# Working out the flags of irregular rows before the slot indices, and leaving their places out of the gather

## The reference

```python
h = jnp.maximum(_layernorm(x, axis=-1), 0.0)
s_i = h @ attn[:d]
s_j = h @ attn[d:]
e = jax.nn.leaky_relu(s_i + s_j.T, negative_slope=0.2)
e = e + jnp.where(adj > 0, jnp.float32(0.0), neg_inf)   # adj: 8192 x 8192 int32
alpha = jax.nn.softmax(e, axis=1)
return x + alpha @ h
```

## Time and profile before

| | |
|---|---|
| median of 3 runs | 822.78 us (821.7 to 823.1) |
| span of the profiled execution | 819.9 us |
| around the span, to the median | 2.9 us |
| DMA engines' share, 60 to 100 us and 600 to 700 us | 1.01 |
| busy: VectorE, ScalarE, GpSimd, TensorE | 615, 534, 505, 380 us |
| bytes moved by DMA | 301.59 MB |

### The profile page before, as it was taken

The page is one execution under the profiler, slowest core; times in us unless marked ns, Lnnn a source line. Parts: engine busy times, 40 slices in busy tenths (PEclk is TensorE's granted clock), DMA queues, the critical chain, the costliest instruction groups (busy, mean ns, idle before and its releaser), DMA issues.

```text
span 819.9 us, 6412 instructions
## 1 busy us (share of the span) xinstructions
PE 379.5 (46%) x1378; PEld 171.4 (21%) x1378; DVE 615.3 (75%) x2028; ACT 534.3 (65%) x410; POOL 505.0 (62%) x526
## 2 busy tenths in 40 slices
PE   1546334444444344344343434444434546653765
PEld 1322011111111011111111101111111215431654
DVE  6898298677768667797778666697689799897831
ACT  4975676676676666766766666676676677764620
POOL 6720777755457767665547677555557667655771
PEclk9776665555555555555555555655555556766768
DMA  8999999999999999999999999999999999981210
GB/s 341 402 411 415 392 404 408 406 414 413 409 407 410 408 405 410 406 410 410 412 406 407 408 406 407 411 410 413 412 413 409 408 411 407 409 348 43 53 37 4
DMA packets 39719, 301.59 MB, mean 368 GB/s; under 512 B 10682, under 2 KB 17149, under 8 KB 22272
## 3 DMA queue, kind: packets, MB, share of 16 engines
q1 hardware_dynamic: 24032, 277.04, 83.1%
q0 software_dynamic: 15360, 23.88, 8.5%
q10 hardware_dynamic: 288, 0.26, 0.1%
HBM read 303.76 MB, written 8.98 MB: 381 GB/s over the span
## 4 chain that ended last, share of the span: by engine, by line
DMA 76%; issue 11%; DVE 5%; ACT 4%; PE 3%; POOL 0%; DVEq 0%; ACTq 0%
DMA adj_ring<-in_adj_dram 75%; ACT sign_ring L613 3%; PE words L1442 2%; DVE one_hot L724 1%; ACT h_all L625 1%; PE words L1406 1%; DMA x_all<-in_x_dram 1%; PE words L1366 0%; DVE cand L769 0%; DVE adj_ring L1142 0%; DVE adj_ring L1138 0%; DVE adj_ring L1146 0%; PE words L1516 0%; POOL out_dram L562 0%; ACT terms L620 0%
## 5 line engine op out<-in xcount | busy, mean ns | idle before, releaser
L613 ACT ACTIVATE sign_ring<-adj_ring,half_neg 128x4096 fp8e3<-128x4096 int32 x128 | 474.9, 3710 | 217.1 <-DMA adj_ring<-in_adj_dram 215.4
L521 POOL DMA_INDIRECT near<-h_table,near_id x384 | 391.8, 1020 | 235.4 <-issue 122.8
L1366 PE MATMUL words<-sign_ring,pack_w 128*128 128x512 bf16 x512 | 225.2, 592 | 354.8 <-ACT sign_ring L613 354.8
L769 DVE MAX8 cand<-words 128x8 f32<-128x256 f32 x256 | 90.9, 417 | 115.4 <-PE words L1366 115.4
L1366 PEld LDWEIGHTS words<-sign_ring,pack_w 128*128 128x128 bf16 x512 | 55.0, 127 | 521.9 <-ACT sign_ring L613 451.6
L954 DVE TENSOR_REDUCE sums<-terms 128x128 f32<-128x1024 f32 x58 | 112.2, 1934 | 2.0
L532 POOL DMA_INDIRECT near_m<-h_table,id_m x64 | 64.5, 1008 | 19.5 <-issue 19.2
L949 DVE TENSOR_TENSOR terms<-near,weight 128x512 f32<-128x512 f32 (+1 forms) x87 | 73.4, 871 | 0.0
L1357 PE MATMUL words<-place,place_w 128*128 128x512 bf16 x128 | 62.1, 586 | 3.6 <-DVE key L861 3.6
L1392 PEld LDWEIGHTS listing<-cand,one_hot 128*128 128x128 f32 x128 | 33.6, 321 | 10.9 <-issue 7.7
L1347 PE MATMUL listing<-h_all 128*1 128x128 f32 x128 | 19.1, 322 | 22.8 <-ACT h_all L625 22.8
(11 more groups left out here) (271 smaller groups left out, 524.3 us busy)
## 6 DMA issues: line engine op xcount, KB each, us to landing
adj_ring<-in_adj_dram SPq DMA_DIRECT2D x128, 2048.0 KB, 24.6
near<-h_table,near_id POOLq DMA_INDIRECT x384, 6.4
h_table<-h_all POOLq DMA_DIRECT2D x4, 1056.0 KB, 14.7
x_all<-in_x_dram SPq DMA_DIRECT2D x4, 1024.0 KB, 9.4
out_dram<-x_all SPq DMA_DIRECT2D x30, 128.0 KB, 23.9
near_m<-h_table,id_m POOLq DMA_INDIRECT x64, 6.4
out_dram<-x_all ACTq DMA_DIRECT2D x2, 128.0 KB, 2.5
adj_ring<-h_table SPq DMA_DIRECT2D x1, 132.0 KB, 2.6
```

What stands on the lines that cost most here:

```text
L521: pool.indirect_dma_start(out=near[:, p % RING, k, :], out_offset=None, in_=table, in_offset=bass.IndirectOffsetOnAxis(ap=near_id[:, p % I ...
L613: nc.scalar.activation(bytes_of, adj_ring[:, n % HALVES, :].rearrange("p (d r i) -> p d r i", r=2, i=WORDS), ACT.Sign, bias=half_neg[:, :] ...
L769: last = nc.vector.max(out=cand[:, p % 2, t % 2, 8 * q:8 * q + 8], in_=words[t % 3][:, q * PART:(q + 1) * PART])
L1366: last = nc.tensor.matmul(at[:, k * BANK:(k + 1) * BANK], pack_w[:, d, :], twins[:, o + k * BANK:o + (k + 1) * BANK], start=False, stop=(d ...
```

## The change

`find_pair` now ends with `missing`. The flag part comes right behind it, then `drop_listed`, which multiplies both rows' codes by `keep` (0 for a flagged row, 1 for any other), and then `place_pair`, which is the rest of the old `find_pair`: merge and indices. The counting of flags is a function of its own, `count_pair`, and stays where `flag_pair` stood, behind the first half of the sums. In pair 0 the three new calls stand in front of the bounds of the lone rows.

```diff
-        FIND = 16
-        FLAG = 6
+        FIND = 17
+        FIND_CODES = 10
+        FLAG = 7
+        FLAG_KEEP = 5
...
                 dve.wait_ge(find, f + 9)
+                nc.vector.tensor_reduce(missing[:, :], invalid[:, p % IDS, :].rearrange("p (a k) -> p a k", a=2),
+                                        AX.X, ALU.add).then_inc(find, 1)
+
+            def drop_listed(p):
+                dve.wait_ge(flagging, FLAG * p + FLAG_KEEP)
+                nc.vector.tensor_tensor(
+                    best_f[:, :].rearrange("p (a k) -> p a k", a=2), best_f[:, :].rearrange("p (a k) -> p a k", a=2),
+                    keep[:, :].unsqueeze(2).broadcast_to([P, 2, 2 * OWN]), ALU.mult).then_inc(find, 1)
+
+            def place_pair(p):
+                f = FIND * p + FIND_CODES
+                dve.wait_ge(find, f + 1)
                 nc.vector.tensor_tensor(best[:, 1, :], best[:, 1, :], best[:, 3, ::-1], ALU.max).then_inc(find, 1)
...
                 nc.vector.tensor_tensor(near_id[:, p % IDS, :], offset[:, :], unused[:, :], ALU.add) \
                     .then_inc(near_id_ready, 1)
-                nc.vector.tensor_reduce(missing[:, :], invalid[:, p % IDS, :].rearrange("p (a k) -> p a k", a=2),
-                                        AX.X, ALU.add).then_inc(find, 1)
...
             def flag_pair(p):
                 f = FLAG * p
                 ts = slice(2 * p, 2 * p + 2)
-                dve.wait_ge(find, FIND * p + FIND)
-                if p > 0:
-                    dve.wait_ge(flags_ready, p)
+                dve.wait_ge(find, FIND * p + FIND_CODES)
                 dve.wait_ge(signed, 4 * p + 4)
...
                 dve.wait_ge(flagging, f + 4)
+                nc.vector.tensor_scalar(keep[:, :], listable[:, ts], 0.0, None, ALU.is_ge).then_inc(flagging, 1)
                 if p >= 2:
                     dve.wait_ge(ranked, p - 1)
...
+            def count_pair(p):
+                f = FLAG * p
+                if p > 0:
+                    dve.wait_ge(flags_ready, p)
...
                 find_pair(p)
+                flag_pair(p)
+                drop_listed(p)
+                place_pair(p)
                 if p < PAIRS - 1:
                     for g in mixes:
                         weigh_mix(g)
                         add_row(g, 0)
-                flag_pair(p)
+                count_pair(p)
```

More of the change, by code:

```diff
@@ L161, in graph_attention_kernel @@
         lacking = sb("lacking", [P, 2], fp32)
+        keep = sb("keep", [P, 2], fp32)
         curve = sb("curve", [P, 2], fp32)
@@ L804, in find_pair @@
                 dve.wait_ge(find, f + 9)
+                nc.vector.tensor_reduce(missing[:, :], invalid[:, p % IDS, :].rearrange("p (a k) -> p a k", a=2),
[8 more added lines that the diff above has]
+                dve.wait_ge(find, f + 1)
                 nc.vector.tensor_tensor(best[:, 1, :], best[:, 1, :], best[:, 3, ::-1], ALU.max).then_inc(find, 1)
-                dve.wait_ge(find, f + 10)
+                dve.wait_ge(find, f + 2)
                 nc.vector.tensor_scalar(power[:, :], best_f[:, 0:SLOTS].bitcast(i32), EXPONENT, None,
@@ L810, in find_pair @@
                                                ALU.is_lt, ALU.mult).then_inc(find, 1)
-                dve.wait_ge(find, f + 11)
+                dve.wait_ge(find, f + 3)
                 nc.vector.tensor_scalar(chunk[:, :], power[:, :], 2.0 / 3 / 2 ** MANTISSA, -2.0 / 3 * FIRST,
                                         ALU.mult, ALU.add).then_inc(find, 1)
-                dve.wait_ge(find, f + 12)
+                dve.wait_ge(find, f + 4)
                 nc.vector.scalar_tensor_tensor(unused[:, :], unused[:, :], 1.0, best_f[:, 0:SLOTS],
                                                ALU.add, ALU.add).then_inc(find, 1)
-                dve.wait_ge(find, f + 13)
+                dve.wait_ge(find, f + 5)
                 nc.vector.scalar_tensor_tensor(offset[:, :], chunk[:, :], float(WORDS), power[:, :].bitcast(fp32),
                                                ALU.mult, ALU.subtract).then_inc(find, 1)
-                dve.wait_ge(find, f + 15)
+                dve.wait_ge(find, f + 7)
                 nc.vector.tensor_tensor(near_id[:, p % IDS, :], offset[:, :], unused[:, :], ALU.add) \
                     .then_inc(near_id_ready, 1)
-                nc.vector.tensor_reduce(missing[:, :], invalid[:, p % IDS, :].rearrange("p (a k) -> p a k", a=2),
-                                        AX.X, ALU.add).then_inc(find, 1)
             def flag_pair(p):
@@ L853, in flag_pair @@
                                             ALU.add).then_inc(flagging, 1)
-                dve.wait_ge(flagging, f + 6)
+                dve.wait_ge(flagging, f + FLAG)
                 nc.vector.tensor_tensor(prior[:, p % 2, 1:2], prior[:, p % 2, 0:1], flag[:, p % 2, 0:1], ALU.add) \
@@ L1215, in _ @@
             find_pair(0)
+            flag_pair(0)
+            drop_listed(0)
+            place_pair(0)
             dve.wait_ge(extreme_spread, 1)
@@ L1227, in _ @@
                                            ALU.is_lt, ALU.max).then_inc(bounds_ready, 1)
-            flag_pair(0)
+            count_pair(0)
             for p in range(1, PAIRS):
```

## The result

The changed kernel takes 823.62 us (median of 20 runs, 821.20 to 825.08), the kernel before 822.22 (20 runs, 819.68 to 824.23). The ratio is 1.0018 with an interval of 1.001 to 1.0026: slower by 0.18%, 1.4 us. 820.9 was forecast, in a range of 819.2 to 823.9. So the time is within the range, but a gain of 1.9 us was forecast and a small loss came. The profiled execution of the changed kernel took 822.9 us with a span of 821.1, where that of before has a span of 819.9: 1.2 us more.

A forecast was written before the change was run, and what follows sets the result against it. The prediction took full DMA engines to bound the stream, followed by a tail of some 70 us. Stream -3.3 and tail +1.4 made -1.9 us: 820.9 against the median of 822.8, range 819.2 to 823.9.

The forecast's parts named there:

- What bounds the stream, and which bytes leave it: Stream up to about 747 us: DMA engines are full; 2610 flagged rows' records, 1.38 MB, leave before it ends.
- The rival in which a flagged row's own first slot is still gathered: Stream: 405 of 2610 records stay, gain 2.8 us, total 821.4; within the 0.22 for less gain or VectorE late.
- The slower rival: Stream: gathers' bytes do not pace it, so only the tail's 1.4 to 2.2 us remain; 824.2 to 825.0, chance 0.14.
- The size of the stream's gain: Stream: leaving out 2610 records brings its end 3.3 us earlier, with 2.2 and 4.0 as bounds.
- The move: Pair's index chain: flags ahead of the merge delay near_id by 1.4 us, hidden in pairs 0 to 30, uncovered in 31.
- VectorE's cover: End of the stream: VectorE's idle time covers two added operations, 0.3 to 0.4 us a pair; about 2.4 us left.
- They are level at 775.58 now, so the tail grows by 1.4: Pair 31: gather chain 1.4 us later, VectorE chain 0.3, so the tail grows by 1.4; bounds 0.3 and 2.2.
- The stall of one gather: Pair 31's last gather took 1.81 us, the first 0.99; without that stall 0.8 us comes back.
- Theory A: From the experiments, tail: pair 31's twelfth gather meets the lone rows' loop's three loads, so the tail grows beyond the move.
- rival B: From the experiments, tail: the last gather lands late by itself, through left-out indices or chance; order costs its plain shift.
- the case in which the stream gains little or nothing: Stream: removed gather bytes do not bring loads forward; the lower edge of this slower case set the range's end, 823.9.

The follow-up runs named there:

- e2_pair31_old: The change in pairs 0 to 30 only, pair 31 in the old order with all places gathered; 819.40 us, ratio 0.9965 to the kernel before.
- e9_drop_more: e2_pair31_old with all rows' places also left out in seven pairs, 6463 records more; 812.80 us, ratio 0.9895 to the kernel before.
- e7_old31_gate: e2_pair31_old with SyncE's wait for pair 31's gathers directly ahead of the lone rows' loop; 818.15 us, ratio 0.9955 to the kernel before.
- e3_order31: The kernel before with the flags ahead of the places in pair 31 alone, nothing left out; 826.19 us, ratio 1.0045.
- e5_order_all: The kernel before with the new order in all pairs, nothing left out of the gathers; 824.69 us, ratio 1.0035.
- e10_before_gate: Control: the kernel before with SyncE's wait for pair 31's gathers ahead of the loop's loads; 821.49 us, ratio 0.9997.
- e6_gate_late: The changed kernel with SyncE's wait for pair 31's gathers behind the reading of the loop's bounds; 820.27 us, ratio 0.9979 to the kernel before.
- e1_gate: The changed kernel with SyncE held until pair 31's last gather lands, before reading the loop's bounds; 821.03 us, ratio 0.9975 to the kernel before.
- e8_gate_mid: The changed kernel with only the loop's adjacency and x tile loads waiting for pair 31's gathers; 821.26 us, ratio 0.9992 to the kernel before.
- e11_gate_x: The changed kernel with only the loop's x tile load waiting for pair 31's gathers; 823.29 us, ratio 1.0018 to the kernel before.

## Why the prediction was wrong, step by step

- **What bounds the stream, and which bytes leave it: right.** q0 22.42 MB and the whole 300.13 were forecast as 22.4 and 300.1. The rival in which a flagged row's own first slot is still gathered falls by the same row: an index below zero moves no record either. The slower rival, in which the gathers' bytes do not pace the stream, falls by e2_pair31_old and e9_drop_more.
- **The size of the stream's gain: perhaps too large, and not settled.** 3.3 us were forecast, 1.3 ns a record, with bounds of 2.2 and 4.0. e2_pair31_old and e7_old31_gate, which change little but the stream, gain 2.9 and 3.7 by their ratios. The other readings are lower. The seven kernels that leave out these records and no others (the changed one among them) have their last sign between 743.75 and 745.15, 744.62 on average; the four that leave out none (before, e3_order31, e5_order_all, e10_before_gate) have it between 746.16 and 747.39, 746.83 on average: 2.2 us. At e9_drop_more's 0.95 ns it would be 2.5. The ratios of e3_order31 and e5_order_all to the changed kernel, which share its meeting, make it 2.2 and 1.4, or 2.5 and 1.7 with the 0.3 us of the two added operations. The 3.06 us at the last maxima of the changed kernel's own profile come near the 3.3 only because 0.85 of them are the clock. Why the loads take longer when the records are gone stays open.
- **The move: right to the hundredth.** 1.4 us forecast, 1.40 in the rows. The sum by the rule of the Trainium skill (VectorE: DVE Perf Modes, The TRN2 errata) had been about 0.6; the trace of the changed kernel does not agree either, each of the small operations takes 0.16 to 0.18 us. The same section of the Trainium skill says that the row with the 58 cycles falls short for a single operation and that its measured fixed term is about 150 cycles, an estimate of 0.16 us at the 0.96 GHz that it gives, and with that the trace agrees; the prediction left it out. That the move is hidden in pairs 0 to 30 is shown by e5_order_all against e3_order31.
- **VectorE's cover: right in that VectorE did not become the bound; its size by luck.** About 2.4 us were worked out to be left ahead of the last tile, and the row has 2.48. But 0.85 of the difference to the 3.72 before is the clock: where the packing ran at the 1.2 GHz level and the order is the same, 3.41 to 3.71 are left (e6_gate_late, e1_gate, e8_gate_mid). The prediction also saw no idle time between 640.03 and 707.64, where the kernel before has 0.55 us at 685.57, and expected none to be left at the release of 707.64, where the changed kernel still has 0.85:

```profile
685.57 1.43 DVE L769 MAX8 cand<-words 128x8 f32<-128x256 f32 x4 [0.55 <-PE words L1366]
```
```profile
705.43 1.43 DVE L772 MAX8 cand<-words 128x8 f32<-128x256 f32 x4 [0.85 <-PE words L1389]
```
- **"They are level at 775.58 now, so the tail grows by 1.4", with bounds of 0.3 and 2.2: this step failed.** From the last maxima to the scores it grew by 4.9 us: 1.4 for the move and 3.5 for the landing. From the last sign to the end of the span it is 76.4 us instead of 72.9, 3.4 more where 1.4 was forecast. The stall of one gather that the prediction reckoned with came back, in the eleventh instead of the twelfth, and pushed the twelfth, so it is the same in both. e1_gate and e6_gate_late bring the landing back to 1.60 and 1.74, and they are 3.5 and 3.2 us faster than the changed kernel by their ratios. With the loads out of the way the tail grows by 1.40 and 1.53, as forecast. Theory A is shown; rival B falls with them, since they keep the order and the indices, and with e3_order31, where no index is changed.
- **What was overlooked** is the three loads of SyncE that stand 2.4 us behind VectorE's L1138. The prediction followed the gathers' chain and VectorE's, saw that they end level, and asked only which would be later. It did not ask what the later one would pass on its way: a margin of 0.31 us between the last gather's issue and the first load was used up by a move of 1.4. The sum had no term for this meeting. By the rows of the two profiles it is -3.1 up to the last maxima (2.2 the stream, 0.85 the clock), +1.4 for the move, +3.5 for the meeting and -0.7 behind the scores: +1.2, against +1.4 by the timed runs. With the meeting away the changed kernel is at -1.7 and -2.1 (e6_gate_late, e1_gate), about the -1.9 forecast. That 823.62 lies within the range of 819.2 to 823.9 is luck: its upper end was set by the case in which the stream gains little or nothing.

That the adjacency tile's load is the larger part of what holds the gather up is shown by e8_gate_mid and e11_gate_x. Through what it does so, a queue in the engines or the strided rows in memory, was not tried.

## What to carry to other kernels

Before moving a chain later, list every transfer that is issued near its end on any queue, with the margin in time; a margin smaller than the move needs a term of its own, here 3.5 us where the margin was 0.31. Such a meeting can be tested, and mended, with one wait on the queue that is not urgent, and a control with the same wait in the old kernel says whether the wait does anything else. A rearrangement that pays by its bytes in a saturated stream need not be made in the last iteration, where nothing is left of the stream to pay it.

## What the runs showed of the hardware that was not expected

- **A strided load beside a gather.** 128 rows of 1024 bytes, 2 MB apart, issued 0.3 us before the end of the gather's issue and 0.7 behind the load of 256 table records, go with a landing of 5.15, 5.26 and 5.06 us (the changed kernel, e11_gate_x, e3_order31) and once of 3.26 (e5_order_all), where it is 1.60 and 1.74 alone (e1_gate, e6_gate_late); the table records alone make it 2.41. Issued 1.0 us behind the end of the gather's issue, the tile's load leaves the landing at 1.63 and 1.88 (before, e2_pair31_old).
- **A gather's issue on GpSimd stretches when it begins just behind the start of a long fp32 operation of VectorE.** The operation is a tensor_tensor of 128x1024, L966 or L1155 of the changed kernel (L949 or L1138 before). In all twelve profiles a gather whose issue begins 0.07 us or more behind its start (up to 1.0) ends 2.07 to 2.11 us behind that start, whatever its own beginning; one that begins with it, within 0.05 us, takes its usual 0.99 to 1.02. In the tail this is the gather that begins some 0.28 us behind L1155 and takes 1.81 us. In the stream the new order moved the gathers over the edge: before, 25 begin with such an operation and 9 behind its start; in the changed kernel 1 and 33, 26 of them at 0.07 or 0.08 us, as here the first gather of a pair,

```profile
148.24 2.00 POOL L524 DMA_INDIRECT near<-h_table,near_id  x1 [3.02 <-DVE near_id L836]
```
```profile
148.17 1.20 DVE L966 TENSOR_TENSOR terms<-near,weight 128x1024 f32<-128x1024 f32 x1
```

  and the gathers' group of the page has 1084 ns in the mean, where the kernel before has 1020 (391.8 us in all):

```profile
L524 POOL DMA_INDIRECT near<-h_table,near_id x384 | 416.3, 1084 | 214.6 <-issue 116.8
```

  It costs nothing here, since e2_pair31_old has the same 1085 ns and is among the fastest. e5_order_all has it too, with nothing left out, so it comes from the order. What in the chip does it was not tested.
- **Records left out of a gather by their index** bring about what their bytes take at the stream's 409 GB/s (1.3 ns for 528 bytes), or less: between 1.7 and 3.7 us for the first 2610, by the reading, and 5.8 for the next 6463, 0.9 ns each. An index below zero moves no record, as one beyond the table: q0 has 19.08 MB in e9_drop_more, the bytes without these records.
